# Two-layer graph network: layer-0 aggregation sums each node tile in a PSUM bank that a register names

## The reference, cut to what matters

```python
ex = jnp.exp(alpha - amax[dst])
denom = jax.ops.segment_sum(ex, dst, num_segments=n)
attn = ex / jnp.maximum(denom[dst], 1e-10)
out = jax.ops.segment_sum(h_src * attn[..., None], dst, num_segments=n)
```

## Time and profile before

| | |
|---|---|
| time, median of 3 runs | 3236.89 us (3231.08 to 3237.75) |
| profiled execution, first to last instruction | 3241.8 us (no other time of it is listed) |
| share of the span: PE, DVE, POOL, ACT | 69%, 63%, 53%, 38% |
| stage sum0, first transfer issued to last add | 764.7 to 1038.9 us |
| bytes moved per window | 264 KB |

### The profile page before, as it was taken

The page is one execution under the profiler, slowest core; times in us unless marked ns, Lnnn a source line. Parts: engine busy times, 40 slices in busy tenths (PEclk is TensorE's granted clock), DMA queues, the critical chain, the costliest instruction groups (busy, mean ns, idle before and its releaser), DMA issues. The chain is left out here.

```text
span 3241.8 us, 48906 instructions
## 1 busy us (share of the span) xinstructions
PE 2228.9 (69%) x10992; PEld 1503.4 (46%) x10993; DVE 2056.2 (63%) x3849; ACT 1246.0 (38%) x3616; POOL 1722.4 (53%) x1802
## 2 busy tenths in 40 slices
PE   3635777767997389948673899997661766654693
PEld 2322333335555356535562677776551444433341
DVE  7587777778788343452677788887682666665221
ACT  2223333326775221234001666665201666652010
POOL 1586777733554301132554777774466777751213
PEclk9867787778999599979766999998765899885555
DMA  4768888874885278825996788886896555530454
GB/s 140 205 181 231 260 263 262 261 235 138 218 219 161 96 254 278 263 90 197 364 396 196 243 274 269 273 276 166 240 291 175 148 147 149 146 107 23 132 152 132
DMA packets 456713, 668.49 MB, mean 206 GB/s; under 512 B 67154, under 2 KB 334092, under 8 KB 456001
## 3 DMA queue, kind: packets, MB, share of 16 engines
q1 hardware_dynamic: 334017, 357.96, 36.3%
q0 software_dynamic: 87248, 261.86, 27.3%
q10 hardware_dynamic: 35296, 46.90, 4.1%
HBM read 491.69 MB, written 176.23 MB: 206 GB/s over the span
## 5 line engine op out<-in xcount | busy, mean ns | idle before, releaser
L1533 POOL DMA_INDIRECT xn<-table,src_col x572 | 595.8, 1042 | 180.6 <-issue 148.9
L1574 PE MATMUL sum_h_ps<-xn,sum_h_hot 128*128 128x261 f32 (+1 forms) x1936 | 526.5, 415 | 192.0 <-DVE xn L1588 128.8
L1574 PEld LDWEIGHTS sum_h_ps<-xn,sum_h_hot 128*128 128x128 f32 x1936 | 369.7, 201 | 341.3 <-DVE xn L1588 251.6
L1092 POOL DMA_INDIRECT arena_a<-table,src_col x264 | 265.6, 1006 | 267.7 <-issue 184.7
L978 POOL DMA_INDIRECT arena_b<-table,src_col x336 | 318.7, 949 | 111.7 <-issue 108.6
L1588 DVE TENSOR_TENSOR xn<-xn,al 128x514 f32<-128x514 f32 (+1 forms) x352 | 243.4, 692 | 167.9 <-DMA xn<-table,src_col 164.0
L1597 DVE TENSOR_TENSOR arena_a<-arena_a,sum_h_ps 128x522 f32 (+1 forms) x440 | 246.1, 559 | 62.1 <-issue 38.2
L1707 PE MATMUL sum_ps<-xn,sum_hot 128*128 128x264 f32 x880 | 245.4, 406 | 31.4 <-DVE arena_a L1730 10.4
L1690 POOL TENSOR_TENSOR xn<-xn,al 128x264 f32<-128x264 f32 x220 | 158.8, 723 | 168.5 <-DMA xn<-edge_h 165.5
L1009 ACT ACTIVATE xn<-score_ps_en 128x512 f32<-128x512 f32 x220 | 131.4, 597 | 291.1 <-PE score_ps_en L995 287.4
L999 PE MATMUL score_ps_hd<-arena_a,score_hot 128*128 x1320 | 238.8, 330 | 0.0
(11 more groups left out here) (516 smaller groups left out, 4628.7 us busy)
## 6 DMA issues: line engine op xcount, KB each, us to landing
xn<-edge_h SPq DMA_DIRECT2D x220, 264.0 KB, 3.2
edge_h<-arena_b SPq DMA_DIRECT2D x84, 528.0 KB
arena_b<-kept SPq DMA_DIRECT2D x66, 516.0 KB, 5.4
xn_t<-edge_rows SPq DMA_DIRECT2D x110, 256.0 KB, 4.6
score_h_hot<-hots SPq DMA_DIRECT2D x220, 128.0 KB, 11.7
kept<-arena_a ACTq DMA_DIRECT2D x40, 516.0 KB, 9.1
xn<-kept SPq DMA_DIRECT2D x66, 257.0 KB
arena_a<-in_f_w SPq DMA_DIRECT2D x16, 1024.0 KB, 8.7
```

The source lines that it names most:

```text
L1092: pool.indirect_dma_start(rows[:, q, s, :], None, table, bass.IndirectOffsetOnAxis(ap=K.src_col[:, w * SUB + s:w * SUB + s + 1], axis=0)). ...
L1533: pool.indirect_dma_start(rows[w][:, s, 0:RW], None, table, bass.IndirectOffsetOnAxis(ap=K.src_col[:, w * SUB + s:w * SUB + s + 1], axis=0 ...
L1574: ins = pe.matmul(ps[:, u, b, 0:part], lhsT=hot[:, w % QH, s, :], rhs=rows[w][:, s, b * part:(b + 1) * part], start=(s == 0), stop=(s == S ...
```

## The change

PE now adds up a node tile over all its windows in one PSUM bank. Eight banks (BANKS) are used in turn: tile t has bank t mod 8. Two tables are made in the projection stage: `K.bank[:, 0, w]`, the tile number plus one, and `K.bank[:, 1, w]`, the bank; `K.tile_end` has the number of windows up to the end of each tile.

- PE loads, for every four windows, four entries of each table into registers. It waits on `s_free` for as many free banks as the first table says, and writes its product to the bank that the second names, without clearing it (start=False). Ahead of the loop it writes zeros into all eight banks by matmuls with a zero tile.
- ACT makes no one-hots any more. Once per tile it loads the tile's end, waits for PE to reach it, copies the bank to the accumulator, and writes zeros into the bank for the tile eight further on, if there is one.
- DVE has no add, no register load and no memset of the accumulator. For each window it makes the one-hots of both halves by two comparisons with a scalar per partition, and then its message. It is no longer fixed at four windows ahead; it may run until it waits for PE's window ten before.
- SP and POOL are as before.

```diff
+def load_four(engine, values, low, high):
+
+    return engine.bass.values_load_multi_w_load_instructions(values, engines=(engine.engine,), min_val=low, max_val=high)[1]
...
             step(dve.tensor_copy(K.window[:, :], t_f[:, :]))
+            step(dve.tensor_scalar(K.bank[:, 0, :], K.window[:, :], 1, None, ALU.add))
+            step(dve.tensor_scalar(K.bank[:, 1, :], K.window[:, :], BANKS - 1, None, ALU.bitwise_and))
+            step(dve.tensor_copy(key_i[:, :], key_t[:, :]))
+            step(dve.tensor_scalar(K.tile_end[:, 0:NT - 1], key_i[:, :], EB.bit_length() - 1, None, ALU.logical_shift_right))
+            step(dve.memset(K.tile_end[:, NT - 1:NT], W))
...
         @block.scalar
         def _(act):
-            NA = len(by_act)
...
+            act.wait_ge(s_none, 1)
+            for t in range(NT):
+                end = act.value_load(K.tile_end[0:1, t:t + 1], min_val=1, max_val=W)
+                act.wait_ge(s_sum, end + Q)
+                act.activation(acc[:, t, :], ps[:, t % BANKS, 0:ROW0], ACT.Copy).then_inc(s_out, 1)
+                act.wait_ge(s_out, t + 1)
+                if t + BANKS < NT:
+                    act.activation(ps[:, t % BANKS, 0:ROW0], none[:, :], ACT.Copy).then_inc(s_free, 1)
...
             pe.sem_inc(s_sum, Q)
+            pe.wait_ge(s_none, 1)
+            for u in range(BANKS):
+                ins = pe.matmul(ps[:, u, 0:ROW0], lhsT=K.ident[:, :], rhs=none[:, :], start=True, stop=True)
+            ins.then_inc(s_free, BANKS)
             with aligned(pe, 0, turns) as i:
                 for j in range(J):
-                    w, q, u = i * J + j, j % Q, j % U2
-                    if j in made:
-                        pe.wait_ge(s_hot, i * len(by_act) + made[j] + 3)
-                    else:
-                        pe.wait_ge(s_hot2, i * len(by_dve) + by_dve.index(j) + 1)
+                    w, q = i * J + j, j % Q
+                    if j % 4 == 0:
+                        needs = load_four(pe, K.bank[0:1, 0, bass.ds(w, 4)], 1, NT)
+                        banks = load_four(pe, K.bank[0:1, 1, bass.ds(w, 4)], 0, BANKS - 1)
+                    pe.wait_ge(s_hot, w + 1)
                     pe.wait_ge(s_msg0, w + 1)
                     pe.wait_ge(s_msg1, w + 1)
-                    pe.wait_ge(s_acc, w + 1)
+                    pe.wait_ge(s_free, needs[j % 4])
                     for s in range(SUB):
-                        ins = pe.matmul(ps[:, u, 0:ROW0], lhsT=hot[:, q, s, :], rhs=rows[:, q, s, :], start=(s == 0), stop=(s == SUB - 1))
+                        ins = pe.matmul(ps[:, bass.ds(banks[j % 4], 1), 0:ROW0].rearrange("p a c -> p (a c)"), lhsT=hot[:, q, s, :], rhs=rows[:, q, s, :],
+                                        start=False, stop=(s == SUB - 1), skip_group_check=True)
                     ins.then_inc(s_sum, 1)
 
         @block.vector
         def _(dve):
             def message(i, j):
                 w, q = i * J + j, j % Q
+                dve.wait_ge(s_sum, w + 1)
+                for s in range(SUB):
+                    ins = dve.tensor_scalar(hot[:, q, s, :], K.iota_row[:, :], K.rel_col[:, bass.ds(w * SUB + s, 1)], None, ALU.is_equal)
+                ins.then_inc(s_hot, 1)
                 dve.wait_ge(s_rows[q], 16 * (i * (J // Q) + j // Q + 1))
...
+            dve.memset(none[:, :], 0.0).then_inc(s_none, 2)
+            with aligned(dve, 0, turns) as i:
                 for j in range(J):
-                    message(i + (j + AHEAD) // J, (j + AHEAD) % J)
-                    if (j + AHEAD) % J in by_dve:
-                        one_hot(i + (j + AHEAD) // J, (j + AHEAD) % J)
-                    add(i, j)
...
+                    message(i, j)
```

More of the change, by code:

```diff
@@ L62 @@
 KQ = 5
+BANKS = 8
 EARLY0 = 26
@@ L226, in items_project_l0 @@
         t_f = st.sbuf("t_f", [P, W])
+        key_i = st.sbuf("key_i", [P, NT - 1], I32)
         t_c = st.sbuf("t_c", [WP, WC])
@@ L1625, in aggregate_l0 @@
     with Stage(prog, "sum0") as st:
-        Q, U2, J = 10, 4, 20
+        Q, J = 10, 20
         AHEAD = 4
@@ L1629, in aggregate_l0 @@
         rows = K.xn[:, :, :].rearrange("p t d -> p (t d)")[:, 0:Q * SUB * ROW0].rearrange("p (q s r) -> p q s r", q=Q, s=SUB)
-        by_dve = [j for j in range(J) if j % 5 == 4]
-        by_act = [j for j in range(J) if j not in by_dve]
-        made = {j: n for n, j in enumerate(by_act)}
         hot = st.sbuf("hot", [P, Q, SUB, P])
[L1634 to L1637, removed]
+        none = st.sbuf("none", [P, ROW0])
+        ps = st.psum("ps", [P, BANKS, 512])
+        s_none = st.sem("none")
         s_rows = [st.sem(f"rows{q}") for q in range(Q)]
-        s_one, s_away, s_hot, s_hot2, s_msg0, s_msg1, s_sum, s_acc = (st.sem(n) for n in ("one", "away", "hot", "hot2", "msg0", "msg1", "sum", "acc"))
+        s_hot, s_msg0, s_msg1, s_sum, s_free, s_out = (st.sem(n) for n in ("hot", "msg0", "msg1", "sum", "free", "out"))
         turns = W // J
@@ L1717, in message @@
                                   ALU.mult).then_inc(s_msg0, 1)
[L1719 to L1738, removed]
-                for j in range(J):
-                    message(i + (j + AHEAD) // J, (j + AHEAD) % J)
-                    if (j + AHEAD) % J in by_dve:
-                        one_hot(i + (j + AHEAD) // J, (j + AHEAD) % J)
-                    add(i, j)
[L1744 to L1750, removed]
+            dve.memset(none[:, :], 0.0).then_inc(s_none, 2)
+            with aligned(dve, 0, turns) as i:
+                for j in range(J):
+                    message(i, j)
 def first_best(dve, step, logits, bias, code, EX, tmp, best, hot, pick):
@@ L2882, in build @@
         K.window = prog.sbuf("window", [P, W], I32)
+        K.bank = prog.sbuf("bank", [P, 2, W], I32)
+        K.tile_end = prog.sbuf("tile_end", [P, NT], I32)
         K.src_s = prog.dram("src_s", [NB, EB], I32)
```

## The result

The changed kernel takes 3246.5 us (median of 13 runs, 3238.8 to 3251.5); in the same runs the kernel before takes 3235.7 (3228.1 to 3242.3). The ratio is 1.0031, with a 95% interval of 1.0022 to 1.0041: slower by 10 to 11 us, a small but measurable loss. Forecast were 3225 us and "faster".

A forecast was written before the change was run, and what follows sets the result against it. PE's sequencer at 1.16 us a window, taken as 1.17 with DVE and POOL close behind, was to bound the kernel: -11 for 220 windows, tail -1.2, start -0.3, projection +0.5, so -12 and 3225 us; range 3199 to 3300.

The forecast's parts named there:

- The bound before: Edge-window stage of the kernel before: DVE's sequencer sets the pace, 1.17 us from add to add, window 1.218.
- The bound after: Edge-window stage after the change: PE's sequencer with its register loads sets the pace, 1.10 to 1.21, middle 1.16 us a window.
- The load of four: PE's sequencer, twice per four windows: loading four registers costs what one costs, 307 ns, with one check per value.
- Rival B: PE's two loads: each further register costs like a first, 1.62 us a window, 3324 us; half price 3273; chance 0.33.
- The handovers between the sequencer's instructions: PE's sequencer, between its steps: 0.04 to 0.06 us each, ten per load block, the 0.04 taken from DVE's tail.
- A window's own part: PE's sequencer, each window besides the loads: wait, bank address, addition, about four handovers, dispatch; 0.38 to 0.40 us, an estimate.
- Rival C: No difference: PE's work per window 0.05 larger, or DVE and POOL lose more; 1.205 to 1.26, 3233 to 3245; chance 0.18.
- DVE and POOL: Window loop: one-hots, message and POOL's multiply, partly excluding each other, need 1.16 or 1.06 us a window; 1.13 taken.
- Rival A: PE's sequencer not the bound: checks merged or cheap, DVE with POOL decides at 1.06 us a window; 3201 us; chance 0.15.
- The transfers: Row transfers' queue in the window loop: 79.6% busy over 276 us read as 1.00 us a window, if 100% is reachable.
- The array 0.90: PE's matmul array in the window loop: 24 records in 5.58 us give 0.90 us a window, running beside the sequencer.
- Tail -1.2: Stage end after PE's last matmul: one ACT copy of a bank replaces DVE's 1.7 us, saving 1.2 us.

The follow-up runs named there:

- unchecked version: The kernel before, with only the bounds check on DVE's register load of the window's tile removed: 3186.5 us against 3237.7, 0.9840.
- Both kernels without the sequencer's bound: Changed kernel with bank-number load unchecked (3205.9 us), and with one checked single value plus an unchecked four-bank load per four windows (0.9926).
- the lean version: Changed kernel with one checked single value and one unchecked four-bank load per four windows, one-hots' node numbers from PSUM, four banks: 3159.8 us, 0.9771.
- the one edit alone: Changed kernel with DVE's one-hots reading the node numbers from PSUM instead of SBUF, four banks in turn instead of eight: 1.0042.
- the other 34 us: Changed kernel with one checked single-value load and one unchecked load of four bank numbers per four windows, node numbers still in SBUF: 0.9926.
- three loads: Changed kernel with a third checked load of four per four windows, its values unused: 3333.6 us, 1.0298.
- the lean loads: One checked single value and one unchecked four-bank load per four windows, on the changed kernel: 0.9926 with node numbers in SBUF, 0.9771 from PSUM.

## Why the prediction was wrong

**The bound before: right.** DVE's sequencer at 1.17 to 1.22, shown by its unchecked version, which won 51 us.

**The bound after: right in kind, too small in size, and this is the step that failed.** The prediction put the sequencer at 1.10 to 1.21, middle 1.16. The terms:

- The load of four: assumed at the price of one, 0.307; it is 0.333. The check bundles: assumed 4 x (151 + 18); they are 4 x (146 to 151 + 18). Both right. Rival B, a price by the register, did not happen.
- The handovers between the sequencer's instructions: 0.04 to 0.06 assumed. They are 0.055 to 0.061 on PE, 0.078 behind the products. The 0.04 came from DVE's tail and doesn't hold for PE. Two blocks are 3.28 us, 0.82 a window; 0.72 to 0.81 was the forecast.
- A window's own part: 0.38 to 0.40 as an estimate, 0.433 measured. It has an addition, two separate waits and a bundle, each with a handover; one wait was counted.
- Sum 1.253, with the branch's 0.02 about 1.27; the first two groups of four at the start, 13.3 us where two periods are 10.1, bring it to 1.29.

From 1.16 to 1.27 the handovers make up about 0.04, the window's own part 0.04, the load 0.01 and the branch, which had no term, 0.02. Each term lay at or over the upper end of what was assumed, and I had taken the middle. The distance between 1.16 and 1.218 was smaller than the doubt about three terms that add up in the same direction for 220 windows: 0.11 us a window is 24 us. Rival C had the right mechanism ("the window's own part on PE is 0.05 larger") but its band of 1.205 to 1.26 was too low as well. That the measured time lies inside the range of 3199 to 3300 says nothing for the sum: its upper part was made for rival B, whose mechanism did not occur.

**DVE and POOL: right, and hidden.** 1.13 was forecast for the pair, with 0.28 for a comparison. Both kernels without the sequencer's bound run at 1.130 and 1.136, and the comparison is 0.27 to 0.28. The sum itself gave 1.16; that the 1.13 taken between its two values fits to the hundredth is luck. That a comparison from SBUF excludes POOL, which no row of before showed, is shown now: 0.27 without POOL, 0.65 in the median beside it, and 344 ns (334 to 367) once it reads PSUM. The Trainium skill ("SBUF — State Buffer", SBUF: two separate sides) had said of 2-port operations that they and GpSimd's lock each other out; the trace agrees, with 0.27 against 0.65.

**Rival A: its candidates were wrong.** With checks out of the way the pair gave 1.13, not 1.06, and instead of the -36 us of that rival 26 and 21 were won.

**The transfers: wrong.** 79.6% of the queue's time over 220 windows was read as a floor of 1.00. At 98% the same bytes go through in 0.90: 303 GB/s against 216, 40% more for a share that is 21% larger. The busy share of a queue that is not full is no measure of what it can do here.

**The array 0.90: right**, reached in the lean version. **Tail -1.2:** measured -1.3, right. **Start -0.3:** the wait for the first matmul is 0.1 shorter (4.3 us from the first transfer's issue, against 4.5). But the first eight windows take 13.3 us where they took 9.4 before, some 3 us more than the slower pace explains; no term stood for that, and its cause was not tested. **Projection +0.5:** 0.27 for the operation behind the new steps, and no later end of the stage beyond 0.1 us; right in kind. **ACT hidden:** right, 16 us of work in 284. The profile puts one gap of PE, 1.2 us at 935.65, down to ACT's zeroing, but the sequencer's wait for the bank took its usual 51 ns there: it is the gap of every group.

**What would show it** did show it: four windows close together and then a gap. The last test that the prediction named, "if PE is idle for DVE or POOL in most windows, the sequencer was not the bound", was a wrong test. The profile does name them, for 72 us, because their events are the last that it sees; the sequencer came to look at them later and, by its own rows, waited 1.3 us.

## What to carry to other kernels

In a loop paced by small steps, add up the sequencer's instructions like an engine's work: each register value that is loaded with bounds costs a check bundle, an assertion and two handovers, on PE some 0.28 us here, and loading four at once saves three loads but no check. If an engine's matmuls come in packs with a gap once per unrolled group, look for what is issued once per group before believing a releaser's name: the wait instructions on the engine's own sequencer say whether it waited (51 ns here when it did not). Where two bounds lie close together, test them in pairs: here the one edit alone gave nothing, the other 34 us, both together 82. And before a change is judged, take the same cost off the kernel before: a check that both kernels pay for is no merit of the change.

## What the runs showed of the hardware

- A register load from SBUF on PE: 307 ns for one value, 333 for four neighbours. The Trainium skill ("Runtime: NRT & Kernel Launch", Instruction fetch mechanics) gives about 200 ns per register for such loads from HBM; these are from SBUF, where three registers more cost 26 ns; no run here loads from HBM.
- PE's sequencer needs 0.055 to 0.061 us between two of its own instructions here, DVE's 0.034 to 0.048 (901.110 + 0.023 to 901.167 in the instruction times of the kernel before is 0.034).
- DVE comparing 128 fp32 columns with a scalar per partition: 0.27 us from SBUF alone and up to 0.73 beside POOL; 0.34 from PSUM, and 0.40 at most in any run with POOL beside it. With the lean loads the form that is slower alone won: 0.90 us a window against 1.13.
- With three loads the granted clock in 880 to 900 us was 0.91, a mean of stretches at 2.4 GHz (889 to 892) and at 1.2 GHz (885 to 888), where all faster versions had 1.00; PE was busy 13.4 of 20 us there, in the changed kernel 14.7.
